# An expert layer on one core: the first two layers with weights loaded and rows streaming, each tile's weights copied to fixed buffers

## What is computed

```
logits = n @ gate_kernel                     # n = layernorm(x), 4096 rows, 8 experts
weights, chosen = top_k(logits, 2); weights = softmax(weights)
for each row and each of its two experts e:
    l1 = n @ w0[e]                           # 128 -> 512
    l2 = n @ w1[e]                           # 128 -> 512
    y  = (silu(l1) * l2) @ wo[e]             # 512 -> 128
out = x + layernorm(sum of the two weighted y)
```

## Time and profile before

| | |
|---|---|
| median of 3 runs | 302.83 us (302.64 to 302.89) |
| the profiled execution's own time | 302.5 us |
| its span in the trace | 300.8 us |
| PE busy | 258.3 us (86%) |
| DVE busy | 203.0 us (67%) |
| ACT busy | 186.8 us (62%) |
| POOL busy | 172.5 us (57%) |

### The profile page before, as it was taken

One profiled execution on the slowest core, in us unless ns is written; L12 is line 12 of the kernel. 1 busy time (PEld: TensorE's weight loads), 2 busy tenths in 40 slices (PEclk: granted clock), 3 DMA queues, 4 the chain that ended last, 5 costly groups with the idle time before them and its releaser, 6 DMA issues.

```text
span 300.8 us, 6844 instructions
## 1 busy us (share of the span) xinstructions
PE 258.3 (86%) x1633; PEld 214.1 (71%) x1633; DVE 203.0 (67%) x944; ACT 186.8 (62%) x451; POOL 172.5 (57%) x195
## 2 busy tenths in 40 slices
PE   0646596879999999999999999999999999999800
PEld 0225263448878698898988889888988988888700
DVE  3787998678597559458755955785653433888745
ACT  3666397327665765767684566666566566568681
POOL 7019577757238775874776577777532333357540
PEclk9995559589999999999999999999999999999985
DMA  5999711302111122112212211343333115602137
GB/s 146 153 384 321 210 50 52 89 29 68 50 47 45 46 74 72 44 56 71 74 44 72 74 46 49 97 108 91 100 81 86 43 31 199 263 17 91 49 99 209
DMA packets 28132, 29.57 MB, mean 98 GB/s; under 512 B 4570, under 2 KB 21180, under 8 KB 28096
## 3 DMA queue, kind: packets, MB, share of 16 engines
q1 hardware_dynamic: 22832, 20.04, 23.4%
q0 software_dynamic: 4544, 8.97, 9.3%
q10 hardware_dynamic: 720, 0.13, 0.3%
HBM read 17.53 MB, written 12.05 MB: 98 GB/s over the span
## 4 chain that ended last, share of the span: by engine, by line
PE 71%; DVE 13%; ACT 6%; POOL 4%; issue 4%; DMA 1%; POOLq 0%; DVEq 0%; ACTq 0%
PE bank L1684 19%; PE bank L1631 10%; PE bank L1632 10%; PE bank L1633 10%; PE bank L1668 10%; PE bank L1626 3%; PE bank L1582 2%; PE bank L1554 2%; ACT sb_row L576 1%; PE bank L1575 1%; POOL expert_rows L457 1%; DMA sb_x<-in_L_attn_x 1%; DVE sb_early L864 1%; PE bank L1566 1%; ACT sb_early L548 1%
## 5 line engine op out<-in xcount | busy, mean ns | idle before, releaser
L470 POOL DMA_INDIRECT pair_rows<-sb_y_rows,sb_y_pair x71 | 70.4, 991 | 60.2 <-ACT sb_y_rows L648 41.6
L457 POOL DMA_INDIRECT expert_rows<-sb_row,sb_place x64 | 64.0, 1001 | 23.8 <-issue 16.6
L1684 PE MATMUL bank<-sb_w_raw,sb_gatedT 128*128 x568 | 75.0, 275 | 0.0
L1684 PEld LDWEIGHTS bank<-sb_w_raw,sb_gatedT 128*128 128x128 f32 x568 | 69.1, 192 | 0.2
L1274 DVE TENSOR_TENSOR sb_w_raw<-bank,sb_w_raw 128x512 f32<-128x512 f32 x71 | 48.9, 689 | 29.9 <-PE bank L1633 21.6
L638 ACT ACTIVATE sb_gatedT<-bank 128x512 f32<-128x512 f32 x71 | 42.3, 596 | 37.0 <-PE bank L1668 36.9
L1631 PE MATMUL bank<-sb_w_parts,sb_x_hi 128*128 x142 | 63.0, 444 | 0.3 <-DVE sb_w_raw L1274 0.2
L1632 PE MATMUL bank<-sb_w_parts,sb_x_lo 128*128 x142 | 56.4, 397 | 0.0
L1633 PE MATMUL bank<-sb_w_parts,sb_x_hi 128*128 x142 | 56.1, 395 | 0.0
L633 ACT ACTIVATE sb_w_raw<-bank 128x512 f32<-128x512 f32 x71 | 42.5, 599 | 7.2 <-PE bank L1633 6.0
L1267 DVE TENSOR_TENSOR sb_x_lo<-bank,sb_x_hi 128x128 fp32r<-128x128 f32 x71 | 20.2, 285 | 35.0 <-ACT sb_x_hi L628 34.7
(11 more groups left out here) (194 smaller groups left out, 358.8 us busy)
## 6 DMA issues: line engine op xcount, KB each, us to landing
sb_taken_rows<-expert_rows SPq DMA_DIRECT2D x71, 65.5 KB, 1.9
sb_w_raw<-in_L_ffn_w SPq DMA_DIRECT2D x2, 2048.0 KB, 15.1
sb_w_raw<-pair_rows SPq DMA_DIRECT2D x3, 1024.0 KB, 7.5
out_dram<-sb_x SPq DMA_DIRECT2D x3, 512.0 KB, 3.8
pair_rows<-sb_y_rows,sb_y_pair POOLq DMA_INDIRECT x71, 2.3
sb_x<-in_L_attn_x SPq DMA_DIRECT2D x4, 256.0 KB, 5.9
expert_rows<-sb_row,sb_place POOLq DMA_INDIRECT x64, 2.4
expert_rows<-sb_pad_row SPq DMA_DIRECT2D x8, 65.5 KB
```

What stands on the lines that cost most here:

```text
L457: pool.indirect_dma_start(expert_rows[:, :], bass.IndirectOffsetOnAxis(ap=place[b % ROWS][:, k, j:j + 1], axis=0), row[b % ROWS][:, j, :], ...
L470: pool.indirect_dma_start(pair_rows[:, :], bass.IndirectOffsetOnAxis(ap=y_pair[group % 2][:, t % PAIRS:t % PAIRS + 1], axis=0), y_rows[slo ...
L1684: last = pe.matmul(p_y[t % 2][:, 0:D], gatedT[t % 2][:, n * P:(n + 1) * P], wo.rearrange("p o d -> p (o d)"), start=(n == 0), stop=(n == F ...
```

## The change

The weights become the operand that is loaded and the rows the one that streams. For every tile, layer 1 is four plain fp32 matmuls of 128 columns, one for each block of 128 of the 512 outputs, and so is layer 2. The results come out already turned (outputs on partitions), so the product of the two goes into layer 3 as it is. ACT copies the tile's `w0` (128x512) into `w0_now`, DVE its `w1` into `w1_now`, two buffers each, a tile ahead; both read the tile's expert into a register for it. The split of weights and rows goes away with all its steps. `last_layer` runs one slot earlier. The first pairs that are read back for the last layernorm get a buffer of their own.

```
-            def layer(to, x_hi, x_lo, first_chunk):
-                w_hi, w_lo = (w_parts[:, bass.ds(first_chunk, FC), part, :] for part in (0, 1))
-                pe.matmul(to, x_hi, w_hi, start=True, stop=False)
-                pe.matmul(to, x_lo, w_hi, start=False, stop=False)
-                return pe.matmul(to, x_hi, w_lo, start=False, stop=True)
+            def layer(to, x, w):
+                for n in range(FC):
+                    last = pe.matmul(to[:, n * P:(n + 1) * P], w[:, n * P:(n + 1) * P], x,
+                                     start=True, stop=True)
+                return last
...
                 n = t % 2
+                pe.wait_ge(c["w0_now"], t + 1)
                 wait(pe, c["silu"], t)
-                layer(p_l1[:], x_hi[n][:], x_lo[n][:], chunks[t]).then_inc(c["l1_ps"], 1)
+                layer(p_l1, xeT[n][:], w0_now[n]).then_inc(c["l1_ps"], 1)
+                pe.wait_ge(c["w1_now"], t + 1)
                 wait(pe, c["gated"], t)
...
+                layer(p_l2, xeT[n][:], w1_now[n]).then_inc(c["l2_ps"], 1)
-
-            def turn_gated(t):
...
@@ PE, the loop @@
                 if is_tile(t - 1):
-                    pe.wait_ge(c["x_lo"], t)
+                    pe.wait_ge(c["xeT"], t)
                 turn_tile(t)
                 if t == 0:
                     pe.wait_ge(a["x1"], 3)
-                    fill(p_y[0], 3)
+                    fill(p_y[0], 2)
                 two_layers(t - 1)
                 a_slot(k, s, 0)
                 chunk_of(t)
-                if t == TILES:
-                    last_layer(t - 3)
-                    turn_gated(t - 2)
-                else:
-                    turn_gated(t - 2)
-                    last_layer(t - 3)
-                if t == 1:
-                    pe.wait_ge(a["x1"], 3)
-                    fill(p_gatedT, 3)
+                last_layer(t - 2)
                 a_slot(k, s, 1)
@@ PE, before the loop: low_part(0) -> fill(p_l1, 6), low_part(1) -> fill(p_l1, 4), low_part(2) gone @@
@@ ACT, the loop @@
                 a_slot(k, s, 0)
+                chunk_of(t + 1)
                 gate_curve(t - 1)
+                fetch_w0(t + 1)
                 a_slot(k, s, 1)
-                gated_turned(t - 2)
                 a_slot(k, s, 2)
@@ ACT, new; round_w x8, take_low x3 and minus_ident are gone @@
+            def fetch_w0(t):
+                if not is_tile(t):
+                    return
+                act.activation(w0_now[t % 2][:].rearrange("p (c f) -> p c f", f=D),
+                               w_raw_chunks[:, bass.ds(chunks[t], FC), :],
+                               ACT.Copy).then_inc(c["w0_now"], 1)
@@ DVE, the loop; rest_part and split_rest are gone @@
+                chunk_of(t + 1)
                 times_gate_curve(t - 1)
+                fetch_w1(t + 1)
                 pairs_of_tiles(t)
@@ DVE, before the loop @@
-            split_rest(LOW_BY_PE, 4)
             top(2)
             choose(2)
-            split_rest(4, 6)
+            start2(3)
             put(2)
+            chunk_of(0)
+            fetch_w1(0)
             offset1(5)
@@ DVE: residual(3) from slot 1 to slot 0 @@
@@ POOL @@
-            for n in range(W_SPLITS // 2):
-                pool.wait_ge(s_w_hi, n + 1)
-                first, size = w_split(n)
-                subtract_hi(pool, first, size // 2)
-                subtract_hi(pool, first + size // 2, size // 2).then_inc(s_w0_lo, 1)
             for b in (0, 1):
                 for n in range(K * G):
                     send_row(b, n)
+            late_power(2, 0, ROOT2, mv2[ROOT2 % 2], sd2[ROOT2 % 2], rs2[ROOT2 % 2])
```

More of the change, by code:

```diff
@@ L174, in sandwich_kernel @@
         y_pair = pair("y_pair", [P, PAIRS], I32)
[L175 to L178, removed]
+        xeT = pair("xeT", [P, P])
+        silu, gated = pair("silu", [P, F]), pair("gated", [P, F])
+        w0_now, w1_now = pair("w0_now", [P, F]), pair("w1_now", [P, F])
         pair_cols = G * K * D
-        pairs_in = [w_raw[:, 4 * F + n * pair_cols:4 * F + (n + 1) * pair_cols] for n in range(6)]
+        pairs_early = sb("pairs_early", [P, 6 * pair_cols])
+        pairs_in = [pairs_early[:, n * pair_cols:(n + 1) * pair_cols] for n in range(6)]
         pairs_in += [early[:, n * pair_cols:(n + 1) * pair_cols] for n in range(2)]
@@ L188, in pairs_of @@
                 return early[:, (first - 6) * pair_cols:(end - 6) * pair_cols]
-            return w_raw[:, 4 * F + first * pair_cols:4 * F + end * pair_cols]
+            return pairs_early[:, first * pair_cols:end * pair_cols]
         def half_of_pairs(b, k):
@@ L633, in gate_curve, with chunk_of @@
                     act.activation(silu[t % 2][:], p_l1[:], ACT.Silu).then_inc(c["silu"], 1)
[L635 to L639, removed]
+            chunks = {}
+            def chunk_of(t):
+                if not is_tile(t):
+                    return
+                if t == 0:
+                    act.wait_ge(s_w_in[0], 16)
+                for p in range(PHASES + 1):
+                    if t == first_tile(p):
+                        act.wait_ge(s_table, p + 1)
+                chunks[t] = act.value_load(tile_chunk_i[0:1, t:t + 1], min_val=0,
+                                           max_val=(E - 1) * FC)
+            def fetch_w0(t):
+                if not is_tile(t):
+                    return
+                act.activation(w0_now[t % 2][:].rearrange("p (c f) -> p c f", f=D),
+                               w_raw_chunks[:, bass.ds(chunks[t], FC), :],
+                               ACT.Copy).then_inc(c["w0_now"], 1)
             def take_y(t):
@@ L1162, in last_new @@
                                                         None, ALU.mult))
-            def split_rest(first, end):
-                for n in range(first, end):
-                    start, size = w_split(W_SPLITS // 2 + n // 2)
-                    dve.wait_ge(s_w_hi, W_SPLITS // 2 + n // 2 + 1)
-                    last = subtract_hi(dve, start + n % 2 * size // 2, size // 2)
-                if end == W_SPLITS:
-                    last.then_inc(s_w1_lo, 1)
             def a_slot(k, s, part):
@@ L1209, in a_slot @@
                 elif s == 0 and k == 0:
-                    sums2(b2)
-                    mean_var(2, b2, mv2, stats2)
+                    residual(b2)
                 elif s == 0:
@@ L1275, in times_gate_curve, with chunk_of, fetch_w1 @@
                                       ALU.mult).then_inc(c["gated"], 1)
+            chunks = {}
+            def chunk_of(t):
+                if not is_tile(t):
+                    return
+                if t == 0:
+                    dve.wait_ge(s_w_in[1], 16)
+                for p in range(PHASES + 1):
+                    if t == first_tile(p):
+                        dve.wait_ge(s_table, p + 1)
+                chunks[t] = dve.value_load(tile_chunk_i[0:1, t:t + 1], min_val=0,
+                                           max_val=(E - 1) * FC)
+            def fetch_w1(t):
+                if not is_tile(t):
+                    return
+                dve.tensor_copy(w1_now[t % 2][:].rearrange("p (c f) -> p c f", f=D),
+                                w_raw_chunks[:, bass.ds(chunks[t] + W_CHUNKS, FC), :]).then_inc(c["w1_now"], 1)
             def pairs_of_tiles(t):
```

102 lines of the change are left out of this document (11 added, 91 removed).

## The result

The changed kernel takes 299.17 us (median of 4 runs, 298.79 to 299.22), the kernel before 302.74 in the same runs: a ratio of 0.988 (95% interval 0.987 to 0.990), 3.6 us faster. The forecast was 7.9 us faster. The profiled execution spans 297.5 us, 3.3 less than before.

What follows compares the result with a forecast made beforehand. PE was taken to bound the loop, with waits across engines ahead of it. From 302.5 profiled: -3.4 loop, +0.4 late products, -4.2 head, -0.7 end gave 294.6, or 294.9 us against the median; range 290.0 to 302.0.

Steps and rivals of the forecast that it cites:

- A slot on PE: PE in the loop: two layers of four fp32 matmuls replace streams and turn; 2.78 against 2.83, -3.4 over 67 slots.
- The head: Start up to tile 4: three steps end earlier, so tile 4 is turned at 67.5: -4.2, bounds -2.5 and -6.5.
- The three steps: In the head: tile 0's turn at 55.0, batch 1's sends ending at 55.7, batch 3's residual at 57.9.
- The end: Behind the last layer 2: PE's wait of 0.78 for the copy of a turned product goes: -0.7.
- the step on ACT and DVE in the loop: Copies and register reads added on ACT and DVE lie beside PE's slot; only products coming late cost, +0.4.
- the +0.4: Cost put on products that come late where DVE's cover is thinnest, in some seven late slots.
- the seven late slots: Slots with the last layernorm's sums, where DVE's cover is thinnest: 2.75 of 2.78 busy with the new copy.
- rival 2: Register reads don't hide: DVE stops 0.6 per tile and sets seven thin slots, +4.0, so 298.5; 9 in 100.
- Rival 1: DVE's copy of `w1` holds up POOL's sends: 0.48 per tile gives 299.6, 0.72 gives 309.2; 19 in 100.
- The loop: The 67 slots from tile 4 to tile 70: -3.4 from PE's shorter slots, +0.4 for late products.
- rivals 2 and 3: Beside rival 2, the third: tile rows or clock hold slots 0 to 3, 4.2 is missing: 299.1; 9 in 100.

Runs made afterwards that it cites:

- the ring opened: Changed kernel with second root ahead of its sends, PE's read behind the layers, other reads ahead except DVE's in eighth slots, ACT's copy behind its second piece: 293.21 us.
- the second experiment: Changed kernel with DVE's and ACT's register reads moved to the start of their slots: 298.87 us, ratio 0.987.

## Why the prediction was right or wrong

- **A slot on PE**: 2.78 forecast, 2.79 measured, loads hidden and the clock at 1.00 from 60 to 280. Right.
- **The head**: -4.2 forecast, -6.3 measured. The three steps came as named: tile 0 at 53.56 (55.0 forecast), the residual at 56.79 (57.9). The 2.1 that the forecast lacks are 1.5 up to tile 2 and 0.6 in slots 2 and 3. Up to tile 2 it is tile 0's turn, 1.4 too late in the sum: PE's ranks of batch 2, which stand ahead of it, start at 52.33 now and at 55.32 before, 3.0 earlier, and I had counted 0.64, one subtraction. To what slots 2 and 3 took together, 6.25, I added 0.85, and they took 6.44, because slot 2, now 2.79, held 0.6 of other time before that I carried along as work (of its 2.53 the streams and the turns are 1.93).
- **The end**: -0.7 forecast; from tile 70's turn to the end of the span it is 21.54, not 23.50: -2.0. I counted the wait and not the last two turns of a product that went with it, 0.44 each, nor the stage that the pipeline lost.
- **What failed** is the step on ACT and DVE in the loop: "All this lies beside PE, whose slot leaves DVE and ACT near 30% idle", and with it the +0.4 and the place I gave it, the seven late slots. Those slots take 2.79 each, the last one 3.28; rival 2, put in the same place, was wrong there as well, though its price was right: a bare read stops DVE for 0.56 to 0.61. The loss was in the fifth and eighth slots of the rounds, 7.1 us. The idle share of an engine says nothing of work that stands in its line behind a wait: the root ahead of that work had a lead over the turn of the slot's tile of 0.67 us in slot 36, 1.95 and 1.97 in slots 20 and 28 and none in slot 12. I had looked only at the first root's idle time, as the slack of POOL, not at when the second root ends against the slot that needs it. Nor had I given the copies and reads a price outside the seven slots.
- **Rival 1** said that POOL closes the round, and a ring through POOL did, but by the 10.3 us that it takes anyway and not by longer sends: with the copy the sends' means rose by 13 and 15 ns over those of the kernel before, where the rival wanted 0.48 a tile.
- The sum of what was measured: -6.3 to tile 4, +4.95 from there to tile 70 (7.1 lost in the ten slots of the table, 0.6 in slots 9 and 68, some 2.8 gained in the others), -2.0 at the end: -3.3 of the span. The loop was forecast at -3.0 in all and is wrong by 8.0; the head and the end, too small by 2.1 and 1.3, hide 3.4 of that. So it is luck that the forecast is off by only 4.3, and that rivals 2 and 3 (298.5 and 299.1) lie near the 299.2 measured: the head did move, and of the late slots only the last lengthened, by 0.3. With the ring opened the kernel takes 293.2, 1.7 under the forecast.

## What to carry to other kernels

Before adding work to an engine that is "30% idle", list the waits in its line and measure, for each, how early it ends against the slot that needs what stands behind it; that lead, not the idle share, is what the addition may use up. When a chain through several engines returns to its start once per round, its length and not the busiest engine sets the round, and moving work from one end of it to the other gains nothing: take it off the ring, as the root ahead of two sends or the copy behind the rows did.

## What the runs showed of the hardware

A copy of 128x512 from SBUF to SBUF on DVE takes 0.42 us (median; the forecast took 0.48), but 11 of the 71 took 0.54 to 0.71. One of those, on DVE's timeline of the changed kernel, beside the sends of POOL, which began one at 161.46 that took 0.98:

```profile
161.98 0.70 DVE L1236 COPY sb_w_now<-sb_w_raw 128x512 f32 x1
...
161.46 0.98 POOL L446 DMA_INDIRECT pair_rows<-sb_y_rows,sb_y_pair  x1 [0.30 <-issue]
```

Others that met a send ran at 0.42 all the same, as that of 177.85 to 178.27 did beside the send begun at 178.03, which took 1.08 and not 0.97. What decides is the moment. In this trace 14 copies begin 0.52 to 0.75 us behind the start of a send; all 14 end 1.19 to 1.26 behind it, whenever they began, and so take 0.47 to 0.71. The other 57 take 0.41 to 0.49, those that begin in the first half us of a send among them. In the other direction, a send that begins 0.07 to 0.24 behind a copy's start takes 1.08 to 1.20. The rule of the Trainium skill that the prediction weighed ("SBUF — State Buffer", section "Who interferes with whom") has a copy and GpSimd lock each other out for a whole instruction. For a send as a whole the trace doesn't agree: of its 0.97 us only a part holds a copy up, by 0.3 at most. Sends are held up by 0.1 to 0.2 in single places, and by 1.5 us over all sends of rows.

A register read on DVE that nothing covers stops the engine for 0.56 to 0.61 us (176.69 to 177.25 in the chain above; 0.61 of idle time ahead of the statistics in the second experiment), though its first step, the load, takes 0.30 as on PE.
